# A recommender tower with a CIN block: the load that spreads the fields' rows over 128 partitions goes through sixteen copies in DRAM

## What is computed

```python
x0 = xk = e                       # (2048, 39, 16) gathered rows
for idx, (W, b) in enumerate([(w0, b0), (w1, b1), (w2, b2)]):
    z = relu(einsum('bhd,bkd,hks->bsd', x0, xk, W) + b[None, :, None])
    if idx != 2:
        xk = z[:, :64, :]; direct.append(z[:, 64:, :])
    else:
        direct.append(z)
z = sum(concatenate(direct, axis=1), axis=-1)          # (2048, 256)
h = relu(concatenate([z, dense_ctx], axis=1) @ W_top1 + b_top1)
y = relu(h @ W_top2 + b_top2) @ W_top3
```

## Time and profile before

| | us |
|---|---|
| median of 3 runs (2804.28 to 2808.67) | 2806.1 |
| span of the profiled execution | 2808.0 |
| PE busy | 2519.5 (90%) |
| DVE busy | 2220.7 (79%) |
| POOL busy | 2153.9 (77%) |
| ACT busy | 1363.8 (49%) |
| mean DMA rate | 166 GB/s |
| hardware queue's packets, share of 16 engines' span | 88.7% |
| mean granted TensorE clock (share of full) | 0.947 |

### The profile page before, as it was taken

The page is one execution under the profiler, slowest core; times in us unless marked ns, Lnnn a source line. Parts: engine busy times, 40 slices in busy tenths (PEclk is TensorE's granted clock), DMA queues, the critical chain, the costliest instruction groups (busy, mean ns, idle before and its releaser), DMA issues.

```text
span 2808.0 us, 32322 instructions
## 1 busy us (share of the span) xinstructions
PE 2519.5 (90%) x8192; PEld 1581.5 (56%) x8192; DVE 2220.7 (79%) x2047; ACT 1363.8 (49%) x1532; POOL 2153.9 (77%) x1350
## 2 busy tenths in 40 slices
PE   1899989899999889999899999999999989998999
PEld 1555555555555555555556556555555555555655
DVE  2788788778778778888788778887878878878883
ACT  2445445445445445445445544554544544544552
POOL 4888778778778778878778878887878887877650
PEclk8999999999999999999999999999999999999999
DMA  7999999999999999999999999999999999999950
GB/s 164 187 162 167 180 164 168 181 160 170 180 163 167 182 166 168 186 167 167 180 167 168 181 173 166 174 182 164 172 181 167 170 181 169 168 180 168 168 117 8
DMA packets 398547, 467.04 MB, mean 166 GB/s; under 512 B 170337, under 2 KB 179553, under 8 KB 398257
## 3 DMA queue, kind: packets, MB, share of 16 engines
q1 hardware_dynamic: 378050, 461.68, 88.7%
q0 software_dynamic: 20480, 5.15, 1.7%
HBM read 457.03 MB, written 9.71 MB: 166 GB/s over the span
## 4 chain that ended last, share of the span: by engine, by line
POOL 55%; issue 22%; SPq 6%; DMA 6%; PE 6%; ACT 1%; DVE 1%; POOLq 1%; ACTq 0%; DVEq 0%
POOL low L459 39%; POOL rows L430 16%; SPq L327 4%; DMA xb<-x_rows 4%; PE z L628 3%; DMA x_rows<-rows 2%; SPq L357 1%; ACT high L776 1%; POOL index L418 0%; SPq L337 0%; PE x L702 0%; PE z L721 0%; PE prod_dve L702 0%; PE z L723 0%; PE z L680 0%
## 5 line engine op out<-in xcount | busy, mean ns | idle before, releaser
L459 POOL TENSOR_TENSOR low<-prod_pool,high 128x1024 fp32r<-128x1024 f32 (+1 forms) x640 | 1529.2, 2390 | 429.2 <-ACT high L776 414.7
L628 PE MATMUL z<-high,w_high 128*128 128x512 f32 (+1 forms) x1920 | 971.0, 506 | 185.1 <-ACT high L776 185.1
L628 PE MATMUL z<-prod_whole,w_whole 128*128 128x512 f32 (+1 forms) x2176 | 1084.1, 630 | 16.1 <-DVE prod_whole L517 16.1
L776 ACT ACTIVATE high<-prod_pool 128x1024 fp32r<-128x1024 f32 (+1 forms) x640 | 676.7, 1057 | 729.4 <-DVE prod_pool L517 676.8
L628 PE MATMUL z<-high,w_low 128*128 128x512 f32 (+1 forms) x1920 | 770.0, 401 | 0.0
L517 DVE TENSOR_TENSOR prod_whole<-xh,x 128x1024 f32<-128x1024 f32 x512 | 621.2, 1213 | 158.2 <-ACT x L753 59.4
L430 POOL DMA_INDIRECT rows<-table,index x640 | 612.7, 957 | 145.7 <-issue 81.5
L628 PE MATMUL z<-low,w_high 128*128 128x512 f32 (+1 forms) x1920 | 642.9, 417 | 83.6 <-POOL low L459 82.3
L628 PEld LDWEIGHTS z<-prod_whole,w_whole 128*128 128x128 f32 (+1 forms) x2176 | 439.8, 202 | 397.2 <-issue 345.0
L517 DVE TENSOR_TENSOR prod_pool<-xh,x 128x1024 f32<-128x1024 f32 x512 | 621.6, 1214 | 11.2 <-POOL low L459 11.2
L628 PEld LDWEIGHTS z<-high,w_high 128*128 128x128 f32 (+1 forms) x1920 | 373.5, 195 | 395.1 <-ACT high L776 197.4
(11 more groups left out here) (45 smaller groups left out, 364.7 us busy)
## 6 DMA issues: line engine op xcount, KB each, us to landing
xh<-x_rows SPq DMA_DIRECT2D x64, 2560.0 KB
xh<-x_rows SPq DMA_DIRECT2D x64, 2432.0 KB
xb<-x_rows SPq DMA_DIRECT2D x128, 546.0 KB
xb<-x_rows SPq DMA_DIRECT2D x64, 468.0 KB
xa<-x_rows SPq DMA_DIRECT2D x192, 78.0 KB
rows<-table,index POOLq DMA_INDIRECT x640
x_rows<-rows SPq DMA_DIRECT2D x256, 20.0 KB
xh<-staged SPq DMA_DIRECT2D x2, 1280.0 KB
```

What stands on the lines that cost most here:

```text
L459: pool.tensor_tensor(low[0:g.rows, g.split_slot, 0:n, :], prod_pool[0:g.rows, g.slot, 0:n, :], high[0:g.rows, g.split_slot, 0:n, :].bitcas ...
L628: return pe.matmul(z[stage][:, :], weights[0:g.rows, table[stage, t], :], src[0:g.rows, i, :], start=t == 0 and weights is not w_low and s ...
L776: act.activation(high[0:g.rows, g.split_slot, 0:n, :], src[0:g.rows, 0:n, :], ACT.Copy).then_inc(high_ready, 1)
```

## The change

`copy_fields` is new: behind `load_pairs`, two transfers from DRAM to DRAM copy the chunk's 20 even rows eight times and its 20 odd rows eight times (row 39, a repeat of row 0, is the twentieth odd one) into `x0_copies`, 16 lines of 20 x 512 floats for each parity. SyncE then waits for layer 2 of chunk c-2 as before, and also for the two copies (`copied`). `load_fields` becomes one transfer to all 128 partitions: each gets one whole line (40 KB, in one run), and eight neighbouring partitions read the same line. The unloaded run of the odd half no longer exists, so GpSimd's two memsets and their semaphore go; the weights of that tile are zero. VectorE's count of `xh_loaded` is one increment of 16 per chunk. With `load_fields(1)` SyncE now waits for the weights' rounding itself, where it waited for GpSimd's second memset, which waited for the same.

```diff
--- before.py
+++ after.py
@@ -43,6 +43,7 @@
 
 PAIR = 2
 G0, GK = -(-T0 // PAIR), TK // PAIR
+COPIES = 16
 STORES = -(-F // GATHERS) + -(-(XROWS - F) // GATHERS)
 WHOLE, BY_POOL, BY_DVE = "whole", "low parts by GpSimd", "low parts by VectorE"
 
@@ -128,6 +129,7 @@
 
     x0_dram = nc.dram_tensor("x0_rows", (XROWS, N), f32, kind="Internal").ap()
     feats_dram = nc.dram_tensor("feats_all", (128, 2, B), f32, kind="Internal").ap()
+    copies_dram = nc.dram_tensor("x0_copies", (2 * COPIES, TK * CN), f32, kind="Internal").ap()
 
     with ExitStack() as stack:
         def sb(name, shape, dt=f32):
@@ -229,13 +231,13 @@
         w0_summed = sem("w0_summed")
         w_rounded = sem("w_rounded")
         w_ready = sem("w_ready")
-        pads_cleared = sem("pads_cleared")
         ids_loaded = [sem(f"ids_loaded{i}") for i in range(2)]
         base_loaded = sem("base_loaded")
         index_ready = sem("index_ready")
         gather_begun = sem("gather_begun")
         gathered = [sem(f"gathered{i}") for i in range(2)]
         stored = [sem(f"stored{i}") for i in range(2)]
+        copied = [sem(f"copied{i}") for i in range(2)]
         xh_loaded = [sem(f"xh_loaded{i}") for i in range(2)]
         x0_loaded = sem("x0_loaded")
         xa_copied = sem("xa_copied")
@@ -340,15 +342,28 @@
                                       ap=[[step, F], [JT * step, n], [1, CN]])
                     sp.dma_start(xb[at, 0:n, :], shifted).then_inc(x0_loaded, 16)
 
-            def load_fields(c, p):
+            def copy_fields(c, p):
+
+
 
                 col = x0_dram[:, bass.ds(c * CN, CN)]
-                step = col.ap[0][0]
+                into = copies_dram[p * COPIES:(p + 1) * COPIES, :]
+                step, line = col.ap[0][0], into.ap[0][0]
                 for hh in range(2):
-                    n = (F + 1 - hh) // 2
-                    spread = bass.AP(tensor=col.tensor, offset=col.offset + hh * step,
-                                     ap=[[0, H], [2 * step, n], [1, CN]])
-                    sp.dma_start(xh[p][hh * H:(hh + 1) * H, 0:n, :], spread).then_inc(xh_loaded[p], 16)
+                    src = bass.AP(tensor=col.tensor, offset=col.offset + hh * step,
+                                  ap=[[0, COPIES // 2], [2 * step, TK], [1, CN]])
+                    dst = bass.AP(tensor=into.tensor, offset=into.offset + hh * (COPIES // 2) * line,
+                                  ap=[[line, COPIES // 2], [CN, TK], [1, CN]])
+                    sp.dma_start(dst, src).then_inc(copied[p], 16)
+
+            def load_fields(p):
+
+                of = copies_dram[p * COPIES:(p + 1) * COPIES, :]
+                line = of.ap[0][0]
+                spread = bass.AP(tensor=of.tensor, offset=of.offset,
+                                 ap=[[line, COPIES], [0, 128 // COPIES], [1, TK * CN]])
+                sp.dma_start(xh[p][:, :, :].rearrange("p t n -> p (t n)"),
+                             spread).then_inc(xh_loaded[p], 16)
 
             def store_feats(c, p):
 
@@ -372,13 +387,17 @@
 
                     wait_made(sp, 0, c - 1)
                 load_pairs(c)
+                copy_fields(c, p)
                 if not known or c >= 2:
 
                     wait_made(sp, 2, c - 2)
                 elif c == 1:
 
-                    sp.wait_ge(pads_cleared, 2)
-                load_fields(c, p)
+                    sp.wait_ge(w_ready, N_SPLIT)
+                    sp.wait_ge(w_rounded, N_GROUPS)
+
+                sp.wait_ge(copied[p], 16 * (c - p) + 32)
+                load_fields(p)
                 if not known or c >= 2:
                     store_feats(c - 2, p)
 
@@ -462,20 +481,12 @@
                 ).then_inc(low_by_pool, 1)
 
 
-            pool.memset(xh[0][H:128, TK - 1, :], 0.0).then_inc(pads_cleared, 1)
-
-            pool.wait_ge(pads_cleared, 1)
             pool.wait_ge(base_loaded, 16)
             for c in range(2):
                 begin_gather(c, c)
                 for j in range(GATHERS):
                     gather(c, j)
 
-            pool.wait_ge(w_ready, N_SPLIT)
-            pool.wait_ge(w_rounded, N_GROUPS)
-            pool.memset(xh[1][H:128, TK - 1, :], 0.0).then_inc(pads_cleared, 1)
-
-            pool.wait_ge(pads_cleared, 2)
             for g in groups(0, 0):
                 if g.kind == BY_POOL:
                     low_parts(g, 0)
@@ -555,7 +566,7 @@
 
             def chunk(c, p):
 
-                dve.wait_ge(xh_loaded[p], 16 * (c - p) + 32)
+                dve.wait_ge(xh_loaded[p], 8 * (c - p) + 16)
 
                 dve.wait_ge(relu_done[0], 3 * c + 2)
                 begun = isinstance(c, int) and c == 0
@@ -578,7 +589,6 @@
                     dve.tensor_tensor(w_low[:, to, :], src, w_high[:, to, :].bitcast(f32),
                                       ALU.subtract).then_inc(w_ready, 1)
 
-            dve.wait_ge(pads_cleared, 1)
             layer0(0)
             over_chunks(dve, chunk)
```

## The result

The changed kernel takes 3115.4 us (3115.1 to 3121.4), the kernel before 2805.2 us beside it: a ratio of 1.111, interval 1.110 to 1.113. It is 11% slower; 2664 us was forecast, 2480 to 2920 as the range.

A forecast was written before the change was run, and what follows sets the result against it. Bound: transfers in SyncE's queue. Period 15.6 (pairs) + 7.2 (copies) + 1.4 (turn) + 12.0 (fields) + 3.3 (stores, wake) = 39.5 us; 65.4 + 62 x 39.5 + 151.2 = 2665.6 us span, so 2664 us; range 2480 to 2920.

The forecast's parts named there:

- The ring of transfers in SyncE's queue: Pairs, fields and row stores follow each other in one queue and set the period, 41.8 us before the change.
- the floor of compute: Shortest period that TensorE and VectorE allow, about 36.1 us per chunk, with 34.1 and 38.3 as its ends.
- Why the fields are slow: Claim that `xh` loads at 205 GB/s because 64 partitions read each run at about the same time.
- The fields' load: Load of `xh` from the 16 copied lines, 5.24 MB at 436 GB/s, taken as 12.0 us per chunk.
- Rival C: The fields' load stays at 205 GB/s, 25.6 us; period 53.1 us, 3509 us in all, slower than before; chance 0.14.
- S: The theory under the prediction: many readers of the same bytes set the fields' rate.
- Copies: The DRAM to DRAM copies behind the pairs: 40 packets on each of 8 engines at 180 ns, 7.2 us.
- The pairs: The pairs' transfers on SyncE's queue, from issue to landing, kept at 15.6 us per chunk.
- Turn and stores: 1.4 us from the fields' issue to first data, and 3.3 us for row stores, landing and SyncE's wake.
- The fields become what compute waits for: Sign of a wrong forecast: VectorE waits for `xh` by more than a microsecond per chunk.

The follow-up runs named there:

- e1: The changed kernel with all 128 partitions reading one 40 KB line, source written as 128, copies kept; 2462.0 us.
- e4: The changed kernel without copies and their wait, one transfer to 128 partitions reading the even rows in 2 KB runs; 2459.8 us.
- e7: The kernel before with the odd half's load issued from ScalarE's queue early, once the rows are stored; 2469.8 us, ratio 0.878.
- e2: The kernel before with each of the 64 partitions per load reading its own stretch of staged weights; 2826.9 us.
- e11: The changed kernel with the step between the 16 lines set to 0, so all partitions read one line in 16 x 8 form; 3115.5 us.
- e9: The changed kernel with the fields' load cut into eight transfers of 16 neighbouring partitions each; 4445.4 us.
- e10: The changed kernel with the fields' load cut into eight transfers, each to every fourth partition of one half; 3066.5 us.
- e5: The kernel before with the two copies and the wait for them added, its fields' loads kept; 3081.1 us, ratio 1.095.
- e3: The kernel before with the odd half's load issued from ScalarE's queue, behind the copy of `xa`; 2633.6 us, ratio 0.939.
- e6b: The kernel before with the two copies added but no wait for the current chunk's copies, its fields' loads kept; 2969.3 us.
- e8: The kernel before with each half's load cut into four parts, issued alternately on SyncE's queue; 2804.2 us beside 2811.6.

## Why the prediction was wrong

- **What bounds the kernel: right.** The ring of transfers in SyncE's queue sets the period before and after, and the floor of compute at 36.1 us is where e1, e4 and e7 end (mean periods 36.1 to 36.2 us; 2455 us was worked out for the span, 2460 to 2470 measured).
- **Why the fields are slow: wrong, and everything else hangs on it.** I compared the 205 GB/s with `feats`' 383 and named the source as what differs. Two things differ: `feats` and the weights also go to 128 partitions in one transfer, `xh` to 64. I named the repeated source without asking about the destination. e2 (own rows, 209 GB/s) and e4 (128 readers, 409 GB/s) show that the source has no part in it.
- **The fields' load: 12.0 us forecast, 25.4 measured.** This is the step that failed. One transfer to 128 partitions does reach full rate if it is dealt out as 128 (e1), but the changed kernel deals it out as 16 x 8, and e11 shows that this alone costs the factor of two. Rival C had the size right (25.6 us), but for S's reason, and I gave it 0.14: its size came right by luck.
- **Copies: 7.2 us forecast, 2.1 measured.** With a DMA share of 0.53 they ran on half of the engines, as forecast, but at 199 GB/s, so some 82 ns per packet (8 engines x 2048 B / 199 GB/s), where I had put 180. Forty such packets are 3.3 us; some 1.2 us of them passed before the pairs were seen. The pairs' rate was the wrong row to price them by. Each of the pairs' transfers writes 39 partitions, and e9 and e10 show how a rate falls with the partitions that are written (the pairs' own rate was not tested so); the copies are written to DRAM., 85 ns, was the right one. With copies of 2.1 us and pairs of 13.5, C's period of 53.1 becomes 45.9 us, about what was measured. By the rule that the prediction cites from the Trainium skill ("DMA: Bandwidth & Descriptors", Rules for kernel authors) an outermost dimension of 8 leaves half of the engines idle; the 0.53 agrees.
- **The pairs: 15.6 us kept, 13.5 measured.** They no longer share the engines with the fields' load. The runs bear this out: in e5, e9, e10 and e11, where the load waits as well, the pairs are seen after 13.6 to 13.7 us in the median, and in e2, e3 and e6b, where it doesn't, after 15.0 to 15.8. The other side of it, 2.0 us of fields' load that no longer pass beside the pairs, was in the forecast, which charged the new load in full.
- **Turn and stores: 1.4 + 3.3 us forecast.** From the copies' end at 1019.0 to the next pairs at 1049.3 are 30.3 us, less 25.4 of fields 4.9: right. The stores' issue was held for 25.18 us behind the long packets, though; "in about 3 us" was wrong, and harmless.
- **The fields become what compute waits for**: 387.0 us in 54 times, the sign that I had named for a wrong forecast.

With the fields' load alone set right (25.4 for 12.0) the forecast's period would have been 52.9 us; the copies (-5.1) and the pairs (-2.1) bring it to 45.7, and 45.95 is the sampled period. The mean of the 62 periods is 46.6, 7.1 more than forecast and so 439 us in all; the two ends (68.5 and 157.4 us, for 65.4 and 151.2) add 9. That is the 448 us by which the span of 3113.9 us passed the forecast's 2665.6.

## What to carry to other kernels

Before a slow load is blamed on its source, ask which partitions the engines write at the same moment: here a load of 64 partitions ran at half rate, a load of 16 neighbours at a quarter, and a broadcast written as 16 x 8 at half, in spite of runs of 40 KB. A copy that makes runs longer pays only if the run's length is what limits, and here 2 KB runs came at 409 GB/s. Where one transfer cannot be dealt out over all 128 partitions, try its halves in two queues, both started early (e7: 12% less time); cutting them finer in one queue did nothing (e8).

## What the runs showed of the hardware

- One transfer to 128 partitions from one 40 KB line, 128 readers: 410 GB/s (e1). The same bytes with the source written as 16 x 8: half rate, 653 us more over the run (e11).
- Two loads of 64 partitions in two queues: 201 GB/s in one stretch, 384 in another, both in flight in both (e7).
- 2 KB packets from DRAM to DRAM on half of the engines move at 199 GB/s, as fast as the half-rate load to SBUF on all 16.
- Issue times on SyncE say nothing of their own cost: six row stores took 25.18 us to issue behind 128 packets of 40 KB, and 3.22 us on the empty queue at the start of the kernel before.
